# The heads' output projection as three half-precision products, the first expert behind the gate, and a new order of the steps

## The reference

```python
x = x + xattn(layernorm(x), ctx)    # causal self attention, then attention on ctx, then a
                                    # hidden layer; three norms with gamma and beta
x = x + attn(layernorm(x))          # 16 heads: qkv = x @ W_attn; softmax, times a decay
                                    # matrix; y = att @ v; return y @ W_proj
x = x + ffn(layernorm(x))           # silu(x1) * x2, norm, sw3; some rows also through the
                                    # best of 8 experts, mixed by a gate
```

## Time and profile before

| what | us |
|---|---|
| median of 3 runs (1572.92 to 1575.41) | 1572.92 |
| the profiled execution's own time | 1579.05 |
| its span, first to last instruction | 1577.2 |
| TensorE busy with matmuls | 1439.5 (91%) |
| VectorE busy | 1070.7 (68%) |
| ScalarE busy | 571.6 (36%) |
| GpSimd busy | 438.8 (28%) |

### The profile page before, as it was taken

One profiled execution on the slowest core, in us unless ns is written; L12 is line 12 of the kernel. 1 busy time (PEld: TensorE's weight loads), 2 busy tenths in 40 slices (PEclk: granted clock), 3 DMA queues, 4 the chain that ended last, 5 costly groups with the idle time before them and its releaser, 6 DMA issues.

```text
span 1577.2 us, 31858 instructions
## 1 busy us (share of the span) xinstructions
PE 1439.5 (91%) x13465; PEld 897.8 (57%) x13465; DVE 1070.7 (68%) x2154; ACT 571.6 (36%) x999; POOL 438.8 (28%) x466
## 2 busy tenths in 40 slices
PE   7078999999999999999999999999999999998678
PEld 3046666656656666566665666666566665664333
DVE  4716676777777777777777777777777777775535
ACT  1412434333434434434333433433443433343221
POOL 0012333333223233323333322333333333322111
PEclk9579999999999999999999999999999999999769
DMA  9143323323333333322332333333332332335410
GB/s 366 60 190 129 113 101 119 130 103 111 135 134 135 134 135 132 126 101 107 133 113 103 128 134 135 135 135 135 130 112 102 121 126 102 115 135 224 139 66 21
DMA packets 36350, 201.32 MB, mean 128 GB/s; under 512 B 4969, under 2 KB 5865, under 8 KB 25713
## 3 DMA queue, kind: packets, MB, share of 16 engines
q1 hardware_dynamic: 36208, 199.29, 34.6%
HBM read 182.24 MB, written 17.04 MB: 126 GB/s over the span
## 4 chain that ended last, share of the span: by engine, by line
PE 45%; DVE 25%; issue 9%; POOL 8%; ACT 7%; DMA 0%; DVEq 0%; SPq 0%; POOLq 0%
POOL rstd L635 8%; PE ps_a L1132 8%; DVE stats L818 7%; PE ps_t L1124 4%; PE ps_a L1166 4%; PE ps_a L1223 4%; PE ps_v L1143 4%; PE ps_t L1143 3%; DVE rows L831 3%; ACT L753 2%; DVE rows L824 2%; PE ps_a L1188 2%; PE ps_t L1254 2%; DVE mv L819 2%; PE ps_a L1178 2%
## 5 line engine op out<-in xcount | busy, mean ns | idle before, releaser
L644 POOL TENSOR_TENSOR act_l<-act_t,act_h 128x512 f16<-128x512 f32 x192 | 216.9, 1130 | 399.0 <-ACT act_t L687 398.9
L635 POOL TENSOR_TENSOR rstd<-var,mhalf 128x1 f32<-128x1 f32 x224 | 170.4, 761 | 563.8 <-DVE var L820 563.8
L679 ACT ACTIVATE act_h<-ps_t,scale 128x512 f16<-128x512 f32 (+1 forms) x160 | 103.6, 648 | 201.9 <-PE ps_t L1124 201.9
L1124 PE MATMUL ps_t<-ident,rows 128*128 128x128 f32 x512 | 83.5, 287 | 44.9 <-DVE rows L824 42.2
L1132 PE MATMUL ps_a<-wproj,act_t 128*128 128x512 f32 x256 | 120.1, 614 | 0.7 <-ACT act_t L749 0.7
L1132 PE MATMUL ps_a<-wcv,act_t 128*128 128x512 f32 x256 | 116.6, 598 | 0.0
L818 DVE BATCH_NORM_STATS2 stats<-rows 128x6 f32<-128x512 f32 x160 | 111.1, 695 | 5.5
L702 ACT ACTIVATE p_n<-rows,ntop 128x128 f32<-128x128 f32 x32 | 12.9, 402 | 269.7 <-DVE ntop L855 269.7
L687 ACT ACTIVATE act_t<-ps_t,scale 128x512 f32<-128x512 f32 (+1 forms) x160 | 103.0, 644 | 0.0
L1143 PE MATMUL ps_a<-w_parts,act_h 128*128 128x512 f16 x384 | 95.9, 387 | 2.1 <-ACT act_h L679 2.1
L1124 PEld LDWEIGHTS ps_t<-ident,rows 128*128 128x128 f32 x512 | 56.7, 143 | 69.2 <-DVE rows L824 66.2
(11 more groups left out here) (246 smaller groups left out, 2910.6 us busy)
## 6 DMA issues: line engine op xcount, KB each, us to landing
ctx_t<-in_ctx_t SPq DMA_DIRECT2D x32, 2056.0 KB, 8.5
ctx_n<-in_ctx_n SPq DMA_DIRECT2D x32, 2048.0 KB
x_in<-in_x SPq DMA_DIRECT2D x32, 256.0 KB, 9.4
ctx_last<-in_ctx_last SPq DMA_DIRECT2D x32, 256.0 KB
x_scratch<-rows SPq DMA_DIRECT2D x32, 256.0 KB, 9.0
out<-rows SPq DMA_DIRECT2D x32, 256.0 KB, 2.2
wattn_f<-in_wattn SPq DMA_DIRECT2D x1, 3072.0 KB, 19.9
wattn<-in_ew SPq DMA_DIRECT2D x6, 512.0 KB, 8.8
```

What stands on the lines that cost most here:

```text
L635: nc.gpsimd.tensor_tensor(rstd[s][:], var[s][:], mhalf[:], ALU.pow).then_inc(rstd_ready[s], 1)
L644: nc.gpsimd.tensor_tensor(act_l[s][:, chunks], act_t[s][:, chunks], act_h[s][:, chunks], ALU.subtract).then_inc(act_l_ready[s], 1)
L679: nc.scalar.activation(act_h[s][:, 0:width // P].rearrange("p c r -> p (c r)"), bank[s][:, 0:width], ACT.Copy, scale=scale[:, k:k + 1]).th ...
L1124: mm = nc.tensor.transpose(out[s][:, c * P:(c + 1) * P], rows[s][:, lo + c * P:lo + (c + 1) * P], ident[:])
```

## The change

The steps for the heads' projection become those of the other split products, `wproj` is split in the weight stage (its raw form lies in the memory of `kbd`, which is cleared afterwards), and the bound of y's size is VectorE's largest value of `wattn` times 512 (in a normalised row the absolute values add up to 512 at most). The counts of `act_h`, `act_l` and `act_t` steps rise from 6, 6 and 7 to 7, 7 and 8 a tile. The new orders are written out in full. In the expert loop `biased(0)` goes behind the coefficients on VectorE, and `gated(i, 0)` behind `coef_t` on ScalarE; TensorE's own list there stays.

```diff
@@ -66,26 +66,26 @@
 
 
 ORDER = {
-    "pe": [(2, "project_k_l"), (3, "turn_z"), (1, "turn_pc"), (2, "project_q_l"), (3, "ffn_out"), (3, "ffn_out_l"),
-        (3, "first_rows"), (1, "context_mix"), (2, "head_scores"), (2, "project_v"), (1, "turn_w"), (0, "turn_xn"),
-        (2, "project_v_l"), (1, "context_out"), (0, "project_self"), (0, "project_self_l"), (2, "head_mix"),
-        (0, "self_scores"), (0, "value_self"), (0, "value_self_l"), (0, "turn_p"), (1, "turn_h2"), (0, "self_mix"),
-        (2, "project_out"), (1, "hidden"), (1, "hidden_l"), (0, "turn_h"), (2, "turn_x2n"), (0, "project_query"),
-        (0, "project_query_l"), (2, "ffn_in"), (0, "context_scores"), (1, "turn_x1n"), (2, "ffn_in_l"),
-        (1, "project_k"), (1, "project_q")],
-    "dve": [(1, "context_total"), (2, "project_k"), (3, "ffn_out"), (0, "xn_moments"), (1, "context_mix"),
-        (0, "turn_xn"), (2, "head_scores"), (2, "head_total"), (2, "head_weights"), (0, "project_self"),
-        (1, "context_out"), (0, "self_scores"), (1, "context_norm"), (0, "self_mix"), (0, "self_norm"),
-        (2, "project_out"), (2, "x2_norm"), (1, "hidden"), (1, "out_norm"), (1, "x1_norm"), (2, "ffn_in"),
-        (0, "context_scores"), (2, "silu"), (2, "z_norm"), (2, "first_rows")],
-    "act": [(3, "ffn_in"), (1, "context_scores"), (3, "turn_z"), (3, "turn_z_t"), (3, "first_rows"), (1, "turn_pc"),
-        (2, "project_k"), (2, "project_q"), (1, "turn_w"), (2, "head_scores"), (2, "project_v"), (0, "turn_xn"),
-        (0, "turn_xn_t"), (0, "self_scores"), (0, "value_self"), (0, "turn_p"), (2, "head_mix"), (1, "turn_h2"),
-        (1, "turn_h2_t"), (0, "turn_h"), (0, "turn_h_t"), (2, "turn_x2n"), (0, "project_query"), (2, "turn_x2n_t"),
-        (1, "turn_x1n"), (1, "turn_x1n_t")],
-    "pool": [(3, "turn_z"), (0, "xn_moments"), (2, "head_scores"), (0, "turn_xn"), (1, "context_out"),
+    "pe": [(3, "turn_z"), (1, "turn_pc"), (2, "project_k_l"), (3, "ffn_out"), (3, "ffn_out_l"), (3, "first_rows"),
+        (2, "project_q_l"), (1, "context_mix"), (2, "head_scores"), (1, "turn_w"), (0, "turn_xn"), (2, "project_v"),
+        (0, "project_self"), (0, "project_self_l"), (1, "context_out"), (2, "project_v_l"), (0, "self_scores"),
+        (2, "head_mix"), (0, "value_self"), (0, "value_self_l"), (0, "turn_p"), (1, "turn_h2"), (0, "self_mix"),
+        (2, "project_out"), (2, "project_out_l"), (1, "hidden"), (1, "hidden_l"), (0, "turn_h"), (2, "turn_x2n"),
+        (0, "project_query"), (0, "project_query_l"), (2, "ffn_in"), (0, "context_scores"), (2, "ffn_in_l"),
+        (1, "turn_x1n"), (1, "project_k"), (1, "project_q")],
+    "dve": [(3, "ffn_out"), (0, "xn_moments"), (1, "context_mix"), (0, "turn_xn"), (2, "head_scores"),
+        (2, "head_total"), (2, "head_weights"), (0, "project_self"), (1, "context_out"), (0, "self_scores"),
+        (1, "context_norm"), (0, "self_mix"), (2, "project_out"), (0, "self_norm"), (2, "x2_norm"), (1, "hidden"),
+        (1, "out_norm"), (1, "x1_norm"), (2, "ffn_in"), (2, "silu"), (0, "context_scores"), (2, "z_norm"),
+        (2, "first_rows"), (0, "context_total"), (1, "project_k")],
+    "act": [(1, "turn_pc"), (2, "project_k"), (2, "project_q"), (0, "turn_xn"), (0, "turn_xn_t"), (2, "head_scores"),
+        (1, "turn_w"), (2, "project_v"), (0, "self_scores"), (2, "head_mix"), (2, "head_mix_t"), (0, "value_self"),
+        (0, "turn_p"), (1, "turn_h2"), (1, "turn_h2_t"), (0, "turn_h"), (0, "turn_h_t"), (2, "turn_x2n"),
+        (0, "project_query"), (2, "turn_x2n_t"), (1, "turn_x1n"), (2, "ffn_in"), (1, "turn_x1n_t"),
+        (0, "context_scores"), (2, "turn_z"), (2, "turn_z_t"), (2, "first_rows")],
+    "pool": [(0, "xn_moments"), (0, "turn_xn"), (2, "head_scores"), (1, "context_out"), (2, "head_mix"),
         (1, "turn_h2"), (0, "self_mix"), (2, "project_out"), (0, "turn_h"), (1, "hidden"), (2, "turn_x2n"),
-        (1, "out_norm"), (1, "turn_x1n"), (2, "silu"), (2, "first_rows")],
+        (1, "out_norm"), (1, "turn_x1n"), (2, "silu"), (2, "first_rows"), (2, "turn_z")],
...
@@ -222,9 +223,10 @@
                     sp.dma_start(wk_t[1][:], a["wck_t"]).then_inc(qk_loaded[1], 16)
                     sp.dma_start(wattn_f[:], a["wattn"]).then_inc(wattn_w3_loaded, 16)
                     sp.dma_start(w3_f[:], a["w3"]).then_inc(wattn_w3_loaded, 16)
+                    sp.dma_start(wproj_f[:], a["wproj"]).then_inc(wattn_w3_loaded, 16)
...
                     sp.dma_start(w12_f[:], a["w12"]).then_inc(w12_loaded, 16)
-                    for name, dst in (("wcv", wcv), ("wproj", wproj), ("mask_self", mask_self),
+                    for name, dst in (("wcv", wcv), ("mask_self", mask_self),
                                       ("mask_head", mask_head), ("decay", decay)):
                         sp.dma_start(dst[:], a[name]).then_inc(late_loaded, 16)
...
                     nc.gpsimd.memset(ones_wide[:], 1.0).then_inc(consts_ready, 1)
+                    pool.wait_ge(wproj_split, 1)
+                    nc.gpsimd.memset(kbd[:], 0.0).then_inc(consts_ready, 1)
                     pool.wait_ge(consts_ready, 5)
 
                 @block.vector
...
                     dve.wait_ge(product_copied, C)
                     largest(K_WQK, flat(wqk_f))
-                    dve.wait_ge(wattn_w3_loaded, 32)
-                    largest(K_WATTN, flat(wattn_f))
+                    dve.wait_ge(wattn_w3_loaded, 48)
+                    step(largest(K_WATTN, flat(wattn_f)))
+                    nc.vector.tensor_scalar(peak[:, K_Y:K_Y + 1], peak[:, K_WATTN:K_WATTN + 1], float(D), None, ALU.mult)
                     largest(K_W3, flat(w3_f))
+                    largest(K_WPROJ, flat(wproj_f))
                     dve.wait_ge(w12_loaded, 16)
                     largest(K_W12, flat(w12_f)).then_inc(peaks_ready, 1)
...
                     with_rows(K_W1, K_W3, K_AFFINE)
-                    with_rows(K_W3, K_PLAIN, K_Z).then_inc(scale_step, 1)
+                    with_rows(K_W3, K_WPROJ, K_Z)
+                    with_rows(K_WPROJ, K_PLAIN, K_Y).then_inc(scale_step, 1)
                     dve.wait_ge(product_copied, 2 * C)
                     largest(K_WCQK, flat(wcqk_f)).then_inc(peaks_ready, 1)
...
+                    remainders(PART_BATCHES[0], 0).then_inc(wproj_split, 1)
...
                 def head_mix(s, r, tile):
                     act.wait_ge(y_done[s], r + 1)
-                    nc.scalar.copy(act_t[s][:].rearrange("p c r -> p (c r)"), ps_t[s][:]).then_inc(y_ready[s], 1)
+                    nc.scalar.activation(act_h[s][:].rearrange("p c r -> p (c r)"), ps_t[s][:], ACT.Copy,
+                                         scale=scale[:, K_Y:K_Y + 1]).then_inc(act_h_ready[s], 1)
+
+                def head_mix_t(s, r, tile):
+                    act.wait_ge(y_done[s], r + 1)
+                    nc.scalar.activation(act_t[s][:].rearrange("p c r -> p (c r)"), ps_t[s][:], ACT.Copy,
+                                         scale=scale[:, K_Y:K_Y + 1]).then_inc(act_t_ready[s], 1)
 
                 def ffn_in(s, r, tile):
...
                     nc.scalar.activation(one[:, 4:5], one[:, 2:3], ACT.Sigmoid).then_inc(shares_ready, 1)
                     act.wait_ge(coef_turned, i + 1)
                     nc.scalar.copy(coef_t[:], ps_gate[0:NE, P:2 * P]).then_inc(coef_t_ready, 1)
+                    gated(i, 0)
                     for k in range(NE):
                         act.wait_ge(e_z_turned, NE * i + k + 1)
                         nc.scalar.copy(z_t.rearrange("p c r -> p (c r)"), ps_z[:, 0:H]).then_inc(e_z_t_ready, 1)
...
                 def project_out(s, r, tile):
                     chain = Chain("project_out", s, r)
                     dve.wait_ge(rows_done[s], 6 * r + 4)
-                    nc.vector.tensor_tensor(rows3[s][:], ps_a[s][:], rows2[s][:], ALU.add).then_inc(x2_ready[s], 1)
+                    nc.vector.scalar_tensor_tensor(rows3[s][:], ps_a[s][:], unscale[:, K_WPROJ:K_WPROJ + 1], rows2[s][:],
+                                                   ALU.mult, ALU.add).then_inc(x2_ready[s], 1)
                     dve.wait_ge(x2_ready[s], r + 1)
...
                     nc.vector.tensor_scalar(pick[:, 3, :], pick[:, 2, :], one[:, 6:7], None, ALU.mult
                                             ).then_inc(coef_ready, 1)
                     dve.wait_ge(coef_ready, i + 1)
+                    biased(0)
                     for k in range(NE):
                         dve.wait_ge(e_gate_ready, NE * i + k + 1)
...
                                                   start=True, stop=True, skip_group_check=True)
                     mm.then_inc(y_done[s], 1)
-
-                def project_out(s, r, tile):
-                    pe.wait_ge(y_ready[s], r + 1)
...
                     "project_q": high_t(ps_t, 4, wattn, 0, whole=5), "project_q_l": low_t(ps_t, 4, wattn, q_done, 0),
                     "project_v": project_v, "project_v_l": low(value_bank, 4, wattn, v_done, 2 * D),
```

(28 more changed lines are left out.)

40 lines of the change are left out of this document (18 added, 22 removed).

## The result

The changed kernel took 1601.68 us (median of 4 runs, 1599.27 to 1606.19), the kernel before 1574.16 beside it (4 runs, 1572.92 to 1577.14): a ratio of 1.0164, interval 1.0148 to 1.0179. It is slower, by 27.5 where 17 were predicted, and inside the range of 1567 to 1604. The profiled execution was the longest of the four, 1606.19, its span 1604.3; the kernel before had a span of 1577.2. The 27.1 between the spans can be laid out.

The account below looks back on a forecast made before the run. It took TensorE as the apparent bound, often held by other engines' chains. Tiles +11, weight stage +7.3, last projection -1.4 and gate +0.2 gave +17 on 1572.92: 1590 us, 1575 to 1602 at 67 in 100.

Parts of the forecast that it names:

- The period: Spacing of head scores in the steady tiles: from 42.87 to 43.2 us, +0.35 each, +11 over 31.
- The walk: Step-by-step reckoning of one period through the new queues, from head scores to next head scores: sum 43.3 us against 42.87.
- Self mix: Its start after the head scores: 16.55 for 16.36, VectorE's chain 0.93 earlier but two ScalarE head-mix activations adding 1.2.
- The product: project_out in half products: 3.44 becomes 1.72 + 0.87, saving TensorE 0.85 a tile, with extra ScalarE, GpSimd and VectorE work.
- The power beside `self_norm`: GpSimd's power ahead of x2n's turn: 0.99 instead of 0.55, sharing SBUF interfaces with VectorE; addition to turn 3.6 for 3.09.
- The three waits: TensorE's waits late in the period: x1n's turn to project_k (1.0), project_q (0.5) and z's turn (0.8).
- The rival by which z's chain is shorter: z's turn comes earlier than walked, period 42.6, total 1571, range 1560 to 1575; 15 in 100.
- X: Time of x1n's turn after the head scores, predicted 31.6 us; z's turn was put 6.4 later.
- TensorE's work decides: Rival: the shorter product sets the tiles' time, -26 us there and 1553 in total; one in ten.
- The table load: ScalarE's load before SiLU, moved ahead of x1n's whole copy: 1.28 without drain; a drain would add 1.4 to z's turn.
- Ahead of the tiles: Weight stage with wproj added: load 2.5, largest value 2.2, step and bound 0.25, with_rows 0.1, remainder 2.3; +7.3 (4.8 to 8.5).
- The end: Behind the tiles: last projection -1.4 (0 to -1.7) from half products, and the reordered gate +0.2 (-2 to +1).

Follow-up runs that it names:

- Experiment 2: The kernel before with the new order alone, keeping the full-float product, old weight stage and old gate: 1622.73 us (one run), period 44.29.
- experiment 3: The changed kernel with ScalarE's head_mix_t moved from ahead of value_self to behind turn_p: 1602.21 us (one run), period 43.51.
- experiment 1: The changed kernel with the order of before, the split product's three new steps put in at their places: 1604.09 us (one run), period 43.48.
- experiment 4: As experiment 1, with VectorE's project_out addition ahead of self_norm: 1572.71 us (7 runs), ratio 0.9977 to the kernel before, period 42.58.
- experiment 5: As experiment 4, with GpSimd's self_mix power ahead of the turn_h2 subtraction: 1566.48 us (one run), period 42.26.
- Experiment 8: The changed kernel with the tail of TensorE's queue as before (x1n's turn, project_k_l and project_q_l put back): 1588.37 us (one run), period 43.0.
- experiment 6: As experiment 5, with a semaphore of its own for the load of wproj: 1565.78 us (5 runs), ratio 0.9918 to the kernel before.
- experiment 7: As experiment 6, with the gate of before on VectorE and ScalarE: 1563.06 us (4 runs), ratio 0.9915 to the kernel before.
- experiment 9: The changed kernel with TensorE's whole queue as before, product still split, other engines' queues new: 1650.78 us (one run), period 44.99.

## Why the prediction was right, and where its terms were off

**The period.** Experiment 2 shows what lengthened it: the new order costs 1.42, and the split pays back 0.79. The walk's offsets held to 0.2 at every step. Predicted and measured offsets: self mix 16.55 and 16.51, project out 17.5 and 17.47, hidden 20.1 and 20.06, h's turn 22.8 and 22.93, x2n's 23.8 and 23.91, query's low part 26.2 and 26.31, x1n's turn 31.6 and 31.79, `project_k` 33.0 and 33.17, z's turn 38.0 and 38.09, next head scores 43.3 and 43.50. The delay starts with VectorE's addition, at 20.33 for 20.2, and ends with 5.41 for 5.3 behind z's turn, where `project_q_l` took back the 0.1 that `ffn_out_l` gave. The 0.2 by which the sum came late, and the 0.1 by which I had rounded it down to 43.2, made +0.35 a period out of what was +0.63 in the steady ones and +0.67 on the average of 30: the term that was mis-sized, +11 for a measured +20.2 in 30 periods. Its upper end was +22. One reading ahead of the walk was wrong: from h's turn to the query's low part I counted 0.6 of waiting that no gap marks, but 0.44 of it is the marked gap at x2n's turn. The walk didn't use it.

**Self mix** came out right by luck, with a wrong reason. I had put two activations of ScalarE in its way; experiment 2 has no second one, experiment 3 has it behind the transposed weights, and self mix stays at 16.51. The place of `value_self_l` in TensorE's queue sets it.

**The product.** That 0.85 goes to TensorE only if no chain holds it is shown from both sides. In the new order it brings 0.79 (experiment 2), in the old one it costs 0.61 (experiment 1), because VectorE's addition stood behind the self norm. The walk had seen this exchange, as "addition at 20.2 (21.30)", but not that the split depends on it.

**The power beside `self_norm`,** 0.99 instead of 0.55, is there in the kernel after, and x2n's turn is where it puts it. The Trainium skill (GPSIMD Engine Reference, Key points) states that GpSimd shares its SBUF interfaces with VectorE instructions of two SBUF inputs. The trace agrees, with 0.99 for 0.55. Experiments 4 and 5 show the other direction as well: VectorE's operation with two SBUF inputs goes from 0.74 to 1.09 beside GpSimd's subtraction.

**The tail of the period.** The three waits were named and are there, 0.78, 0.43 and 0.58. Experiment 8 puts two of them back and gains 0.5 a period. The rival by which z's chain is shorter is false: power and subtraction stand in the order that was walked, and z's turn comes at X + 6.3 for 6.4. That the power alone holds it there is not shown: VectorE, which I had not walked here, reached the norm's second half about 0.16 after the power's end.

**TensorE's work decides** is false: TensorE's busy time fell by 0.59 in a period that grew by 0.63.

**The table load.** The row's price held, as shown above: 1.28, and the activation 0.01 behind it. The Trainium skill (ScalarE: Activation LUTs, What ACT_TABLE_LOAD costs) puts a drain of some 1.38 with the load. By that, as an estimate, z's turn would have come at about 39.5; it came at 38.09.

**Ahead of the tiles.** +7.3 was predicted up to the first tile's statistics; measured is +7.4 (83.41 against 76.01). VectorE's timeline of the kernel after, against the earlier trace rows:

```profile
35.69 6.55 DVE L269 TENSOR_REDUCE peak<-wattn_f 128x1 f32<-128x6144 f32 x1 [8.22 <-DMA kbd<-in_wproj]
...
43.47 2.28 DVE L269 TENSOR_REDUCE peak<-kbd 128x1 f32<-128x2048 f32 x1
...
72.64 2.34 DVE L324 SCALAR_TENSOR_TENSOR wproj<-kbd,scale,wproj 128x2048 f16<-128x2048 f32 x1
...
83.41 0.69 DVE L831 BATCH_NORM_STATS2 stats<-x_in 128x6 f32<-128x512 f32 x1 [4.30 <-DMA x_in<-in_x]
```

The load costs 2.67, the largest value 2.28 and the remainder 2.34. What I had not foreseen is the stretch from there to the first head scores, 74.4 against 72.2. It goes with TensorE's granted clock and not with the change. One by-window row of this stretch each of the kernel after, of experiment 2 (the new order without the split) and of experiment 3, which differs from the kernel after by one moved activation, with the granted clock third from the end:

```profile
83.41:157.81 74.40, 55.28 (x483) 38.49 (x487) 27.04 (x60) 15.80 (x32) 12.51 (x13) 0.81 0.39 151
```

```profile
76.30:150.42 74.12, 55.03 (x483) 38.22 (x486) 27.04 (x60) 15.81 (x32) 12.51 (x13) 0.81 0.39 151
```

```profile
84.03:154.30 70.27, 51.14 (x482) 35.13 (x486) 27.03 (x60) 15.82 (x32) 12.53 (x13) 0.88 0.40 158
```

The eleven traces follow it closely: at 0.88 the stretch took 70.2 and 70.3 (experiments 4 and 3), at 0.85 70.8 (experiment 1), at 0.84 72.7 twice (6 and 7), at 0.82 72.2 (before), at 0.81 73.7 to 74.7 (after, 2, 5, 8 and 9). Kernels with the split and with the new order stand at either end. So the 2.2 is not the change's; what sets the clock from one execution to the next was not found.

**The end.** Behind the last head scores I had -1.2 and measured +0.1; the last period, which I had counted like the others, took 2.8 less than before. That belongs to the new order: experiment 2, without the split, has 40.97 there for its 44.29, experiment 1, in the old order, 43.24 for 43.48. TensorE's timeline of the kernel after, the last projection and the gate, against the earlier trace rows:

```profile
1515.89 3.60 PE L1157 MATMUL ps_a<-wproj,act_h 128*128 128x512 f16 x8 [0.81 <-ACT act_h L756]
1519.28 1.91 PE L1166 MATMUL ps_a<-wproj,act_l 128*128 128x512 f16 x4
...
1542.93 6.59 PE L1316 MATMUL ps_a<-wqk,act_t 128*128 128x512 f32 x8
...
1552.79 0.27 PE L1326 MATMUL ps_e<-ident,pick 128*8 128x128 f32 x1
...
1558.29 0.69 PE L1333 MATMUL ps_t<-ident,p_n 128*128 128x128 f32 x2 [3.76 <-DVE p_n L1107]
```

The three half products take 5.30, from 1515.89 to 1521.19, for 6.34: 3.39 for the high half and 1.91 for the low one, where three quarters of 6.34 had been 4.8. That is -1.0 for -1.5. The float product had a granted clock of 0.58 (0.50 up to 1492.00, 0.73 from 1493.00 on), the half products 0.50 (1.2 GHz) throughout. The gate was predicted at +0.2 and measured at +0.06 (experiments 4 and 7); TensorE's wait for the coefficients goes, as named, and its wait for the first expert's rows grows (1.41 to 3.75).

Two things that I had not counted take the -1.0 back. VectorE's timeline of the kernel after has a wait for the expert's rows from memory, at the first operation on them:

```profile
1535.88 0.69 DVE L1028 BATCH_NORM_STATS2 stats<-x_in 128x6 f32<-128x512 f32 x1 [0.81 <-DMA x_in<-x_scratch]
```

The kernel before has none there, and from z's turn to the turn of these rows it is 4.27 for 3.78, +0.5. The other is the clock: the products of the first two experts took 6.59 and 5.43 for 6.22 and 5.28, +0.5.

Together: +20.2 - 2.8 in the tiles for +11, +7.4 + 2.2 ahead of them for +7.3, +0.1 behind for -1.2. The sign and the mechanisms are as predicted; the period carries the miss.

## What to carry to other kernels

Where each engine's queue is written out by hand, a shorter product can lose its whole saving if the operation that takes its result stands behind others in the next engine's queue: here one exchange on VectorE turned the same split from 1.7% slower than the kernel before into 0.2% faster, and one on GpSimd with a semaphore of its own for the new load took it to 0.8% faster. Measure a new order and a new product apart: the order alone cost 1.42 a period here, and the product won back 0.79 (experiment 2). Walk the period step by step and keep the sum that the walk gives: an error of 0.1 counts 31 times. Don't put one engine's queue back alone and read the result as the price of that queue.

## What the runs showed of the hardware that was not expected

- VectorE's scaled norm on 128x512 with SBUF inputs took 0.74 with no GpSimd subtraction beside it and 1.09 beside one of 128x512 (experiments 4 and 5), the same on 128x256 0.47 (before) and 0.92 (after); the prediction had only GpSimd's side of it.
- The first expert's product (8 float matmuls of 128x512) took 6.59 in the kernel after, 6.22 before, 5.10 in experiment 6 and 3.68 in experiments 4, 5 and 7. The granted clock from the turn of the experts' rows to this product was 0.50 (1.2 GHz) in the first three, and 0.92, 0.81 and 1.00 (2.4 GHz for most or all of it) in the other three. It is worth up to 3 us here, far more than the reordered gate, and what decides it between kernels that differ little was not found.
